# A graph layer on one core: GpSimd's gathers wait for products instead of landings, a shorter start, and an earlier last tile

## The reference

```python
msgs = edge_weight[:, None] * xn[dst]
h = segment_sum(msgs, src, 3125)                       # the graph part
x = x + (h @ Wg.T + bg) + mix(xn)                      # mix: linear attention over all nodes, 8 heads,
...                                                    #   two layer norms, a 256-256-256 gelu MLP
f = layernorm(x)
logits = mean(f, nodes) @ Wr + br                      # one route for all nodes: two of 8 experts
x = x + ffn(f)                                         # two experts 256-512-256, gelu, a layer norm
```

## Time and profile before

| what | value |
|---|---|
| median of 3 runs | 953.44 us (951.49 to 954.23) |
| the profiled execution | 949.6 us, of which the span of its instructions is 947.9 us |
| busy in the span | PE 781.0, DVE 682.2, POOL 582.3, ACT 415.1 us |
| gathers | 440, first at 114.93, last at 762.64 us |
| mean granted clock of PE | 0.932 |

### The profile page before, as it was taken

The page is one execution under the profiler, slowest core; times in us unless marked ns, Lnnn a source line. Parts: engine busy times, 40 slices in busy tenths (PEclk is TensorE's granted clock), DMA queues, the critical chain, the costliest instruction groups (busy, mean ns, idle before and its releaser), DMA issues.

```text
span 947.9 us, 14062 instructions
## 1 busy us (share of the span) xinstructions
PE 781.0 (82%) x4353; PEld 638.3 (67%) x4353; DVE 682.2 (72%) x1939; ACT 415.1 (44%) x1008; POOL 582.3 (61%) x648
## 2 busy tenths in 40 slices
PE   7879868888887788878877877768777777999997
PEld 5649866776776456556655656556655646999997
DVE  8889859999887555445555867668676687666676
ACT  2736755675773133313332323222223326666551
POOL 3847578878887577676666666666666610333453
PEclk9998979999899899989997989989898899999999
DMA  7210033233333333334233333233332311000000
GB/s 244 79 61 2 10 98 88 84 91 88 89 87 100 95 96 113 88 92 121 84 108 89 111 90 113 86 90 113 91 112 86 110 32 56 13 23 24 23 30 31
DMA packets 38994, 76.88 MB, mean 81 GB/s; under 512 B 9811, under 2 KB 22536, under 8 KB 38920
## 3 DMA queue, kind: packets, MB, share of 16 engines
q0 software_dynamic: 21120, 57.70, 20.9%
q1 hardware_dynamic: 17800, 18.29, 6.1%
HBM read 69.48 MB, written 6.48 MB: 80 GB/s over the span
## 4 chain that ended last, share of the span: by engine, by line
PE 42%; DVE 12%; issue 8%; POOL 6%; ACT 2%; DVEq 1%; DMA 0%; POOLq 0%
PE bank L2021 14%; PE bank L1812 10%; DVE X L1301 6%; POOL ARENA L707 6%; PE bank L1863 5%; PE bank L1870 2%; DVE ARENA L1289 2%; PE bank L1937 2%; PE bank L1926 2%; PE bank L1878 1%; PE bank L1770 1%; PE bank L1649 1%; PE bank L1940 1%; DVE ST L1033 1%; DVE KS L1351 1%
## 5 line engine op out<-in xcount | busy, mean ns | idle before, releaser
L707 POOL DMA_INDIRECT ARENA<-xg_rows,ARENA x440 | 424.3, 964 | 197.8 <-issue 121.1
L1812 PE MATMUL bank<-ARENA 128*128 128x256 f32 x880 | 246.6, 420 | 90.2 <-issue 43.9
L1301 DVE TENSOR_TENSOR X<-bank,X 128x256 f32 x440 | 185.3, 421 | 182.2 <-PE bank L1812 167.8
L1812 PEld LDWEIGHTS bank<-ARENA 128*128 128x128 f32 x880 | 171.4, 207 | 141.0 <-issue 57.2
L1289 DVE TENSOR_SCALAR ARENA<-iota,ARENA 128x128 f32<-128x128 f32 x440 | 157.7, 363 | 0.0
L1770 PE MATMUL bank<-OIA,ASA 128*128 128x128 f32 x676 | 93.0, 304 | 16.3 <-issue 6.1
L1770 PEld LDWEIGHTS bank<-OIA,ASA 128*128 128x128 f32 x676 | 91.5, 220 | 19.9 <-issue 18.8
L828 ACT ACTIVATE OIA<-iota,LANE 128x128 f32<-128x128 f32 x286 | 85.9, 389 | 13.9 <-PE bank L1770 13.6
L996 ACT ACTIVATE HF<-bank,FB 128x262 f32<-128x262 f32 (+1 forms) x96 | 46.8, 487 | 42.1 <-PE bank L2021 22.6
L872 ACT ACTIVATE NK<-bank 128x256 f32<-128x256 f32 x25 | 9.6, 383 | 116.3 <-PE bank L1863 116.3
L2021 PE MATMUL bank<-QH,W1L 128*128 128x262 f32 (+1 forms) x192 | 55.9, 291 | 2.3 <-DVE W1L L1548 1.7
(11 more groups left out here) (320 smaller groups left out, 1540.6 us busy)
## 6 DMA issues: line engine op xcount, KB each, us to landing
ARENA<-xg_rows,ARENA POOLq DMA_INDIRECT x440, 2.8
FW1A<-in_exp_w SPq DMA_DIRECT2D x8, 512.0 KB, 3.8
xg_rows<-XGS SPq DMA_DIRECT2D x12, 256.0 KB, 2.1
out<-YO SPq DMA_DIRECT2D x24, 128.0 KB, 1.7
X<-in_x SPq DMA_DIRECT2D x1, 1664.0 KB, 12.4
X<-in_x SPq DMA_DIRECT2D x1, 1536.0 KB, 8.1
FW<-in_exp_w SPq DMA_DIRECT2D x2, 512.0 KB, 4.6
QKVW<-in_qkv_wT SPq DMA_DIRECT2D x1, 768.0 KB
```

What stands on the lines that cost most here:

```text
L707: pool.indirect_dma_start(RING[:, at, :], None, xg_dram, bass.IndirectOffsetOnAxis(ap=SIX[:, c:c + 1], axis=0)).then_inc(gathered[at // HA ...
L1301: V.tensor_tensor(xt, pair_bank(pair)[:, half * C:(half + 1) * C], xt, ALU.add).then_inc(x_added, 1)
L1812: ins = T.matmul(pair_bank(pair)[:, u * C:(u + 1) * C], SEL[:, t % 2 * HAND + k, :], RING[:, h * HAND + k, :], start=True, stop=True)
```

## The change

- From column 124 on, ahead of the first gather of every hand h, POOL waits for the products of the first pair of hand h - 2 (`begun`). The landing waits are taken out.
- In sort B POOL issues 6 gathers ahead of its first `group_columns`, where it issued 14; then it is 4 columns past the hand that PE takes in that turn, where it was 8.
- The third table piece is multiplied after tile 21 of `xg` and not 23, and DVE reads the first piece ahead of its last `slot_rank`.
- The order of tiles for the experts becomes 0 to 5, 24, 6, 7 to 23. Tiles 24 and 6 are turned ahead of the zero matmuls at the router (3 and not 4 of these), copied between the router's exponentials, and tiles 7 and 8 are normalised there too; before, tiles 24, 8 and 9 were normalised after the table load for the gelu.
- At the end of loop B the statistics and the update of the short last tile come two pairs earlier.

```diff
-        AHEAD = 8
-        EL_AFTER, LB_AFTER, ED_AFTER, BID_AFTER = (16, 16, 18), (17, 17, 19), (19, 20, 23), 24
+        AHEAD = 7
+        EL_AFTER, LB_AFTER, ED_AFTER, BID_AFTER = (16, 16, 18), (17, 17, 19), (19, 20, 21), 24
...
+        AHEAD_OF_PAIRS = 4
-        BREATHS = set(range(COLS_A, 2 * B_FIRST, 2 * HAND)) | set(range(2 * B_FIRST, COLS, 8))
...
-        TURNS = list(range(AHEAD)) + [TILES - 1] + list(range(AHEAD, TILES - 1))
+        TURNS = list(range(AHEAD - 1)) + [TILES - 1, AHEAD - 1] + list(range(AHEAD, TILES - 1))
+        AT_ROUTER = TURNS[AHEAD - 1:AHEAD + 1]
...
+            def begun(t):
+                pair = t * PER
+                pool.wait_ge(chunk_mm[pair % 2], pair // 2 + 1)
...
-                so_far = min(COLS_A, 2 * upto(n + 1) + 8)
+                so_far = 2 * upto(n + 1) + min(2 * n, AHEAD_OF_PAIRS)
...
             for c in range(issued, COLS_A):
+                if c % HAND == 0:
+                    begun(c // HAND - 2)
                 gather(c)
             pool.wait_ge(slots_ready, 2)
             for c in range(COLS_A, COLS):
-                if c in BREATHS:
-                    pool.wait_ge(*landed(c - 1))
+                if c % HAND == 0:
+                    begun(c // HAND - 2)
...
-            ffn_normalise(range(6, 8))
+            ffn_normalise(AT_ROUTER)
+            ffn_normalise(with_block(0))
             router_exp(0, NE)
+            ffn_high(AT_ROUTER)
             router_exp(1, NE)
             router_exp(2, TOPK)
             act.activation(R[0:1, 1, 5:6], zeros[0:1, 0:1], ACT.Gelu)
-            ffn_high(range(6, 8))
-            ffn_normalise([TILES - 1])
...
-            for g in range(EARLY_RANKS):
+            for g in range(EARLY_RANKS - 1):
                 slot_rank(g)
+            piece_columns(0)
+            slot_rank(EARLY_RANKS - 1)
+            piece_columns(1)
+            piece_columns(2)
             group_columns()
...
-            columns(p + 8, p + 10)
             b_out(PAIRS, (0,))
-            columns(p + 10, p + 11)
-            b_update(PAIRS, (0,), p + 11)
-            columns(p + 11, COLS // 2)
+            columns(p + 8, p + 9)
+            b_update(PAIRS, (0,), p + 9)
+            columns(p + 9, COLS // 2)
...
-            split_hidden(0, 0, range(0, 4))
-            low_parts(range(6, AHEAD))
-            split_hidden(0, 0, range(4, 8))
-            low_parts([TILES - 1])
+            low_parts(AT_ROUTER)
+            split_hidden(0, 0, range(0, 8))
...
-            stay_busy(bank[4], 4)
-            ffn_transpose(range(6, 8))
+            ffn_transpose(AT_ROUTER)
+            stay_busy(bank[4], 3)
...
-            ffn_transpose([TILES - 1])
             ffn_transpose(with_block(0))
```

More of the change, by code:

```diff
@@ L514, in pair_bank @@
             return bank[(2 if pair < PAIRS_A else 6) + pair % 2]
-        def landed(c):
-            r, at = divmod(c, RC)
-            return gathered[at // HAND], 16 * (r * HAND + at % HAND + 1)
         def per_chunk(m, G, n):
@@ L999, in _ @@
             for b in range(NBLK):
-                ffn_normalise(with_block(b))
+                if b:
+                    ffn_normalise(with_block(b))
                 hidden(b, range(NH))
-                if b == 0:
-                    ffn_high([TILES - 1])
                 ffn_high(with_block(b))
@@ L1127, in _, with piece_columns @@
             V.tensor_copy(DD[:, :, 0:1], DC[:, SA:SETS, 0:1]).then_inc(dd_ready, 1)
-            def group_columns():
[L1130 to L1134, removed]
+            def piece_columns(k):
+                lo, hi = PIECES[k]
+                dve.wait_ge(lb_ready, k + 1)
+                dve.wait_ge(ed_done, k + 1)
+                V.scalar_tensor_tensor(out=DCB[:, lo:hi], in0=LB[:, lo:hi], scalar=local_p[:, 0:1],
+                                       in1=piece_bank(1, k)[:, 0:hi - lo], op0=ALU.is_le, op1=ALU.mult).then_inc(ed_read, 1)
+            def group_columns():
                 dve.wait_ge(ed_read, len(PIECES))
```

## The result

The changed kernel takes 891.2 us against 953.84 us before (951.49 to 955.65, 4 runs): a ratio of 0.9344 [0.9318, 0.937]. The 891.2 is the median of 890.0, 890.31, 892.1 and a fourth execution of 2543.05 us, which the ratio leaves out; without it the median is 890.31. The profiled execution takes 890.31 us and its span 888.6, which is 59.3 less than before.

The account below looks back on a forecast made before the run. The prediction took POOL's gathers, gaps and landing waits to bound the kernel. Gains of 2.0 + 5.5 + 12.5 + 3.5 + 25 + 1 + 2 = 51.5 us took 953.4 to 902 us; range 885 to 917, widened to 886 to 924.

Parts of the forecast that it names:

- What bounds the kernel: First gather to last: POOL works or waits for a landing for all 648 us, 61 us of them landing waits.
- Third table piece: Ahead of the first gather: DVE has the piece near 60.9 instead of 63.13; -2.0 us.
- Sort B: Sort B: PE's groups come 5.0 us sooner, column 132 at 307.3 instead of 312.83; -5.5 us.
- Loop A and the passage: Loop A at 12.62 us a step, less 1 for the gate: -12.5; passage between loops, two landing waits: -3.5.
- rival 4: From column 132: POOL stops at the gate at every hand and the ring drains; 26 us slower, 979; chance 0.04.
- Loop B: Loop B: 17.9 us per 14 columns, nearest POOL's 17.5, so 227.6 instead of 252.5 us; -25, bounds -30 and -14.
- 16.8 / 0.90 = 18.7: Loop B: PE's and DVE's own step of 16.8 us at full clock would be 18.7 if all slowed at clock 0.90.
- Last tile and experts: End of loop B: statistics off DVE's last adds, -1 us; experts: ACT's copies and normalising moved into router waits, -2 us.
- Rival 1: Both loops: PE and DVE bind at about 13.2 and 18.9 us a step, halving the gain; 922 us; chance 0.22.
- Rival 2: Gathers: landings slow down when nobody waits; only the start and experts gain, 5 us; 948 us; chance 0.04.
- Rival 3: Loop B: DVE instructions reading SBUF twice hold gathers 1.0 us each, giving back 48 us; 950 us; chance 0.04.

Follow-up runs that it names:

- e7: The changed kernel, gate kept, with 24 landing waits put back from column 248 on, every 8th column: 932.95 us, ratio 0.9786.
- e5: The changed kernel, gate kept, with sort B's gathers as before (14 first, then 8 columns past PE's hand): 889.73 us, ratio 0.933.
- e6: The changed kernel with only every second column gathered from column 150 on, PE multiplying old rows for the others: 886.72 us, ratio 0.9317.
- e4: The changed kernel without the gate, keeping its smaller lead in sort B: 884.09 us, ratio 0.9286.
- e1: The kernel before with the gate in place of the 34 landing waits, all else as before: 894.92 us, ratio 0.9393.
- e9: The changed kernel with the gate kept only up to column 275: 888.05 us, ratio 0.9308.
- e10: The changed kernel with the gate only from column 276 on: 890.15 us, ratio 0.9346.
- e12: The changed kernel run once more, nothing changed: 892.31 us, ratio 0.9346.

## Why the prediction was right, and where it was off

The measured 891.2 lies inside the range of 886 to 924, 11 below the forecast of 902.

**What bounds the kernel.** Right: POOL's work plus its gaps was the whole path from the first gather to the last. e7 shows it with one suspected cost put back: each landing wait counts at its full price. Two slips in its figures change little: of the 34 landing waits one was a plain gap, so that 57.4 should be 58.9; and the bounds of its terms with the least gain add up to 20.3 us, which would put the upper end at 933 and not at 917.

**Third table piece.** -2.0 predicted, -2.1 measured at the first gather. The piece's wait fell to 1.77 us, as this row of DVE says; its counterpart is in the earlier trace rows.

```profile
61.40 0.73 DVE L1135 SCALAR_TENSOR_TENSOR ARENA<-ARENA,local_p,bank 128x500 f32<-128x500 f32 x1 [1.77 <-PE bank L1739]
```

**Sort B.** -5.5 predicted, -3.8 measured at column 132 (306.97, with the 2.1 of the start taken off); the forecast for this column was near 305. The wait that was taken out counted in full. PE's groups did come about 5 us sooner, as the last group and pair 57 show (before: the earlier trace rows; 2.1 of the distance is the earlier start):

```profile
287.62 1.60 POOL L691 TENSOR_TENSOR ASA<-LHA,EPC 128x832 f32<-128x832 f32 x1
...
298.16 1.89 PE L1818 MATMUL bank<-ARENA 128*128 128x256 f32 x8
```

The step that failed is that column 132 comes sooner with them. By POOL's own account, 132 steps and 19 groups, 165.5 + 28.7 = 194.2 us lie between the first gather and column 132, which is the time measured, and e5 has the same with the groups late. The prediction itself said that POOL's total work is the same, and where POOL is the bound only its total counts.

**Loop A and the passage.** -12.5 and -3.5 predicted. On the eleven steps from which the -12.5 was worked out, -8.9 were measured; that the whole loop gave -11.6 is luck, from 2.7 ahead of its first step, which the forecast left out. The passage gave -3.9. Steps between L1884 are 12.6 us in six cases of eleven, and 14.3 in two. The prediction took every step above 12.6 as one in which a hand came late; some were, the two of over 16.5 before, but e6 shows that the average of 13.04 stays when POOL has half the work. The gate held POOL three times there, for 1.2, 1.9 and 2.0 us, within the 1 to 5 us allowed, though oftener than once or twice.

**The gate at the way into loop B** was not foreseen. The prediction took a first product as about 1.0 us, after distances from loops A and B, and looked for bites in loop A. The largest, 3.25 us, is at column 276, where POOL comes before PE has the product of pair 132. It is a wait of rival 4's kind, at one place instead of 51.

**Loop B.** -25 predicted, with -30 as its bound, and -36.3 measured. This is the term that was mis-sized, and both halves of it failed.

- "The larger of POOL's 17.5 and PE's and DVE's own" counted all 178 columns at POOL's pace. When PE starts column 262 at 496.40, POOL has already issued up to column 275. What is left is 499.74 - 496.40 = 3.3, then 205.3 for POOL's gathers from column 276 to the last, then 7.5 until the last adds end. That is 216.2 us, and 17.0 for 14 columns. A ring that enters a loop with a stock and leaves it nearly empty lets the loop run faster than its producer. It did so before, too: column 276 started at 522.00, and 4.4 + 240.6 + 7.5 = 252.5.

```profile
522.00 0.95 POOL L707 DMA_INDIRECT ARENA<-xg_rows,ARENA  x1 [0.30 <-issue]
```

  So the forecast held a pace without the stock (17.5 or 17.9) against a measured one with it (19.9). Of the 36.3 us gained, 35.3 lie between column 276 and the last, where 20 landing waits at 1.79 make 35.8.
- "16.8 / 0.90 = 18.7" made PE's and DVE's pace a possible bound above POOL's. e6 measures it as 16.5, at a clock of 0.99. The divisor went away with the stops: 0.96 in the changed kernel's loop, and 0.91 again in e7.

Had I put POOL's account straight into the total (2.0, then 61.1 less 1 to 5 for the gate, then 2 at the end), I would have come to 60 to 64 us, or 889 to 893. Taking 17.9 for the pace gave away ten of them.

**Last tile and experts.** -1 and -2 predicted; -1.8 measured behind the last adds. The last tile's part was to show ahead of their end, and isn't seen there: from the last gather to the end of the adds it takes 7.5 us, as before. The table load's neighbours, as the earlier trace rows, in ACT's timeline:

```profile
734.94 0.20 ACT L968 ACTIVATE R<-R 1x2 f32<-1x2 f32 x1 [1.58 <-DVE R L1560]
735.16 1.28 ACT L982 ACT_TABLE_LOAD   x1
736.46 0.20 ACT L982 ACTIVATE R<-zeros 1x1 f32<-1x1 f32 x1
736.64 0.47 ACT L999 ACTIVATE HF<-bank,FB 128x256 f32<-128x256 f32 x1
```

The last exponential and the first gelu are 1.70 us apart; before, they were 3.63 apart. So ACT's part gained 1.9, as worked out. But that exponential comes 22.4 us after the last adds instead of 20.8, so 1.6 of it is paid back in front. Which of the moved instructions takes it wasn't tried.

**The rivals.** Rival 1 (PE and DVE bind at once) is out for loop B of the changed kernel, which gained three times what it gave; it becomes true at e4, at 16.7 a step, not 18.9. For loop A its pace of about 13.2 was nearer to the measured 13.04 than the forecast's 12.62. Rival 2: landings are 2.8 us as before. Rival 4: 7.4 us of extra stop at the gate in all, not 1.4 at each of 51 hands.

Rival 3: the median gather is 946 ns as before, although DVE's work is denser. But DVE does hold gathers, as the long ones show:

```profile
341.68 1.86 POOL L703 DMA_INDIRECT ARENA<-xg_rows,ARENA  x1 [0.30 <-issue]
...
342.04 0.68 DVE L1363 TENSOR_TENSOR QT<-QR,EQ 128x512 f32<-128x512 f32 x1
```

The gather ends 0.82 us after L1363, which reads two tensors in SBUF. In the changed kernel 17 gathers of 440 last longer than 1.05 us, and 15 of them end 0.82 us after such a DVE instruction (ten after L1363, four after the update of `X` at L1442). The Trainium skill's page SBUF — State Buffer, section "SBUF: two separate sides", says that a DVE instruction with two inputs in SBUF and a GpSimd instruction that reads SBUF exclude each other on a shared pair of ports for the whole instruction. This trace agrees. The other direction shows as well: each of the seven selections of more than 0.6 us (up to 2.24) ends 0.09 to 0.10 us after a `group_columns` ends. What rival 3 had wrong is the size. The 17 long gathers lose 6.2 us in all (before, 13 lose 6.8), since most gathers miss such a moment, and the updates of `X` cost the ones that they hit 0.15 to 0.2 us and not 1.0.

**Left open.** The gate slows loop B's steps by about 0.5 us. What that costs the whole kernel is known only as 2 to 7 us, by the ratios of three pairs of kernels, none of which settles it by its own interval. Loop A has three steps of 13.8 to 14.3 us in e6 too, so it isn't for want of gathers that they are long; what makes them so wasn't tried.

## What to carry to other kernels

Add up the engine that feeds a ring from its first transfer to its last, with the fixed gap behind each instruction and each wait. If the sum fills the stretch, each wait taken out counts in full, whatever the busy share says, and the total follows from that sum better than from a pace guessed for each loop. Count the ring's stock at both ends of the loop. A wait that only holds the producer back (for landings, or for products beyond what the ring needs) should first be tried at zero. Then remove half of the producer's work in an experiment: it tells at once how far the next bound is (in loop B 0.7 us a step, in sort B 15 us in all, in loop A nothing).

## What the runs showed of the hardware

- PE's granted clock in loop B rose from 0.90 to 0.96 once PE's stops for late gathers were gone, and the same products took 17 us less of PE's time. The share of full speed lies between the two levels, 1.2 and 2.4 GHz, so this is a mean over stretches at either. With the landing waits back in loop B it fell to 0.91 (e7).
- 163 gathers in a row took POOL 205.3 to 206.7 us, 1.26 to 1.27 each, in the seven traces where neither a landing nor a full ring stopped it for long (the changed kernel, e1, e4, e5, e9, e10, e12), although PE and DVE stood at other places of their work beside them.
- DVE and POOL hold each other up. In the changed kernel 15 gathers ended 0.82 us after a DVE instruction with two inputs in SBUF, up to 1.2 us late (2.10 instead of 0.95), and seven selections ended 0.09 to 0.10 us after a `group_columns` on POOL, up to 1.9 us late (2.24 instead of 0.34).
